# A two-layer transformer on one NeuronCore: two weight splits, the four-bit weight parts, the zeroing of the experts' rows and a count product in other places

## The reference

```python
def _L0_attn_ref(x, Wq, Wk, Wv, Wo):
    q = jnp.einsum('bsd,ed->bse', x, Wq)
    k = jnp.einsum('bsd,ed->bse', x, Wk)
    v = jnp.einsum('bsd,ed->bse', x, Wv)
    kvt = jnp.cumsum(k * v, axis=-2) * denom
    vhat = q * kvt
    return jnp.einsum('bse,fe->bsf', vhat, Wo)
...
# _L0_ffn_ref: a shared expert of 352 columns, and 8 experts of 176 columns of which each token takes 2
scores = jax.nn.sigmoid(xf @ gate_w.T)
topk_w, topk_idx = jax.lax.top_k(scores, TOP_K)
shared_out = jax.nn.silu(xf @ shared_wg.T) * (xf @ shared_wu.T) @ shared_wd.T
...
routed_out = (topk_w[..., None] * picked).sum(axis=1)
return (shared_out + routed_out).reshape(B, S, D)
...
# _L1_ffn_ref: weights stored in four bits, with a scale for each 32
vals = NVFP4_LUT[idx]
vals = vals.reshape(N, K // block, block) * scales[:, :, None]
...
x = L0_attn_x
xn = _layernorm(x, axis=-1)
x = x + _L0_attn_ref(xn, ...) + _L0_ffn_ref(xn, ...)
xn = _layernorm(x, axis=-1)
x = x + _L1_attn_ref(xn, ...) + _L1_ffn_ref(xn, ...)
```

## Time and profile before

| | us |
|---|---|
| median of 3 executions | 723.02 |
| lowest, highest | 722.76, 724.7 |
| the profiled execution | 726.48 |
| its span in the profile | 724.7 |
| PE busy | 666.8 |
| DVE busy | 503.4 |
| ACT busy | 391.8 |
| POOL busy | 364.0 |

### The profile page before, as it was taken

The page is one execution under the profiler, slowest core; times in us unless marked ns, Lnnn a source line. Parts: engine busy times, 40 slices in busy tenths (PEclk is TensorE's granted clock), DMA queues, the critical chain, the costliest instruction groups (busy, mean ns, idle before and its releaser), DMA issues.

```text
span 724.7 us, 12634 instructions
## 1 busy us (share of the span) xinstructions
PE 666.8 (92%) x4346; PEld 524.1 (72%) x4346; DVE 503.4 (69%) x964; ACT 391.8 (54%) x691; POOL 364.0 (50%) x299
## 2 busy tenths in 40 slices
PE   7999978899979799999899999999999989999996
PEld 4877756888878677776577767667777767776774
DVE  6888696558656858583966686495858487568755
ACT  4654323456544654753855492675465286449273
POOL 2333874857565734462646264364537163426453
PEclk9999998999999999999999999999999999999999
DMA  8527585698876567020024021003303000302100
GB/s 306 175 97 231 167 297 190 209 305 267 281 232 218 199 226 233 16 74 2 1 74 124 9 56 35 1 2 119 85 5 84 2 1 30 75 15 53 36 2 30
DMA packets 66802, 82.72 MB, mean 114 GB/s; under 512 B 7090, under 2 KB 50354, under 8 KB 66738
## 3 DMA queue, kind: packets, MB, share of 16 engines
q1 hardware_dynamic: 63156, 73.39, 32.0%
q0 software_dynamic: 3072, 8.39, 3.6%
q10 hardware_dynamic: 512, 0.13, 0.1%
HBM read 40.34 MB, written 28.84 MB: 95 GB/s over the span
## 4 chain that ended last, share of the span: by engine, by line
PE 54%; DVE 15%; issue 10%; ACT 10%; SPq 4%; POOL 2%; DMA 2%; another core or an unknown queue 1%; ACTq 1%; DVEq 0%; POOLq 0%
PE acc L660 4%; PE acc L662 4%; PE acc L661 4%; PE ring L660 3%; PE pm L662 2%; PE pm L661 2%; PE pm L660 2%; PE ring L661 2%; PE ring L1001 2%; PE ring L662 2%; PE ring L1007 2%; SPq L623 2%; PE pv L660 2%; PE pv L662 2%; PE pv L661 2%
## 5 line engine op out<-in xcount | busy, mean ns | idle before, releaser
L1606 POOL TENSOR_TENSOR hl<-hf,hh 128x512 fp32r<-128x512 f32 (+1 forms) x76 | 101.3, 1335 | 227.2 <-ACT hh L1286 226.8
L1286 ACT ACTIVATE hh<-hf 128x512 fp32r<-128x512 f32 (+1 forms) x76 | 47.6, 630 | 78.7 <-DVE hf L2160 60.8
L660 PE MATMUL acc<-hh,wh 128*128 128x512 f32 (+1 forms) x168 | 71.8, 427 | 2.9 <-POOL hl L1606 2.9
L2224 DVE TENSOR_REDUCE mx<-ring 128x2 f32<-128x512 f32 (+1 forms) x96 | 61.5, 682 | 8.4 <-PE ring L1007 8.4
L662 PE MATMUL acc<-hl,wh 128*128 128x512 f32 (+1 forms) x168 | 66.2, 394 | 0.0
L661 PE MATMUL acc<-hh,wl 128*128 128x512 f32 (+1 forms) x168 | 66.2, 394 | 0.0
L2160 DVE TENSOR_TENSOR hf<-hf,pv 128x512 f32<-128x512 f32 x64 | 43.6, 681 | 30.6 <-PE pv L662 26.1
L1751 POOL TENSOR_TENSOR pl<-act,ph 128x512 f16<-128x512 f32 x32 | 42.1, 1316 | 36.5 <-ACT ph L1501 29.7
L1478 ACT ACTIVATE hf<-pm 128x512 f32<-128x512 f32 x56 | 33.4, 596 | 43.2 <-PE pm L662 37.4
L660 PE MATMUL pv<-xh,wh 128*128 128x512 f32 x128 | 53.5, 418 | 0.0
L662 PE MATMUL pv<-xl,wh 128*128 128x512 f32 x128 | 50.6, 395 | 0.0
(11 more groups left out here) (294 smaller groups left out, 2047.1 us busy)
## 6 DMA issues: line engine op xcount, KB each, us to landing
w4s<-w4hl SPq DMA_DIRECT2D x16, 512.0 KB
ws<-qs SPq DMA_DIRECT2D x12, 512.0 KB, 5.4
qT<-qp SPq DMA_DIRECT2D x96, 64.0 KB
kT<-kp SPq DMA_DIRECT2D x96, 64.0 KB
xs<-yg SPq DMA_DIRECT2D x2, 2944.0 KB, 12.7
ys<-act SPq DMA_DIRECT2D x22, 256.0 KB
stage<-w SPq DMA_DIRECT2D x8, 608.0 KB, 4.9
xh<-xs SPq DMA_DIRECT2D x12, 256.0 KB
```

The costliest lines, as they stand in the source:

```text
L660: pe.matmul(o, w_hi, x_hi, start=first, stop=False, skip_group_check=True)
L1286: a.activation(h_parts(n)[0][0:rows, :], hf[0:rows, n % 2, :], ACT.Copy).then_inc(s_hh, 1)
L1606: return pool.tensor_tensor(dst, src, hi.bitcast(F32), ALU.subtract)
L2224: v.tensor_reduce(mx[:, i, h0:h0 + nh], ring[j % 2][:, :].rearrange("p (n k) -> p n k", n=nh), AX.X, ALU.max).then_inc(s_mx, 1)
```

## The change

Five things move. (1) The lo parts of pieces 11 and 12 are made by VectorE instead of GpSimd: 11 with piece 10 in group 1, 12 in group 2 behind `gated` of tile 1. (2) GpSimd's `w4_parts(0)` waits until the lo parts of the fourth group's vhat are there (`s_vhl`), and the parts 0 to 3 stand one place later each among the splits and scatters; `codes(0)` and the first two `scales_hi` come earlier, in group 2, tile 1, and `codes(4)` and `codes(5)` two steps of the loop later, `w4_out` of 1 to 5 likewise. (3) `clear(0)` is issued ahead of `piece(12)`. (4) GpSimd's first four tiles of rows go out together, then two, then two. (5) `counts(1)` stands ahead of `shared_down(3, 0)`, before it stood behind it.

```diff
-        lo_of = {0: [0, 2, 4, 6, 8, 10, 14], 1: [1, 3, 5, 7, 9, 11, 12, 13]}
+        lo_of = {0: [0, 2, 4, 6, 8, 10, 11, 12, 14], 1: [1, 3, 5, 7, 9, 13]}
...
             piece(11)
-            piece(12)
             sp.wait_ge(s_zero, 1)
             clear(0)
+            piece(12)
...
             w4_out(0)
-            w4_out(1)
...
-                    w4_out(2)
+                    w4_out(1)
                     rows_load(4)
...
-                if q in (4, 7, 10):
-                    w4_out(q // 3 + 2)
+                if q in (4, 5, 10, 11):
+                    w4_out(2 + q % 2 + q // 10 * 2)
...
+                if g == G - 1:
+                    counts(1)
                 shared_down(g, 0)
                 if g < G - 1:
                     qkv(g + 1, 0, 0)
-                if g % HG == 1:
-                    counts(g // HG)
+                if g == 1:
+                    counts(0)
...
+                    if g == 2 and t == 1:
+                        scales_hi(0)
+                        scales_hi(1)
...
-                if g == 2:
-                    scales_hi(0)
-                    scales_hi(1)
...
-                if q == 1:
+                if q == 3:
                     scales_hi(2)
...
-            rows_out_to(0, 0, 1)
-            weights(11)
-            rows_out_to(0, 2)
+            rows_out_to(0, 0, 1, 2, 3)
             split_h(6, ST_M[0])
-            rows_out_to(0, 3, 4)
+            rows_out_to(0, 4, 5)
             split_h(7, ST_M[1])
             split_h(8, ST_M[2])
-            weights(12)
-            rows_out_to(0, 5, 6, 7)
-            pool.wait_ge(s_wlo[1], lo_of[1].index(12) + 1)
+            rows_out_to(0, 6, 7)
+            pool.wait_ge(s_wlo[0], lo_of[0].index(12) + 1)
+            pool.wait_ge(s_wlo[1], lo_of[1].index(9) + 1)
+            pool.wait_ge(s_vhl, 2 * G)
             w4_parts(0)
+            split_h(9, ST_M[0])
             w4_parts(1)
-            split_h(9, ST_M[0])
-            w4_parts(2)
             split_h(10, ST_M[1])
             split_h(11, ST_M[2])
             rows_out_to(1, 0, 1)
+            w4_parts(2)
             w4_parts(3)
-            rows_out_to(1, 2, 3)
+            rows_out_to(1, 2, 3, 4, 5)
             w4_parts(4)
-            rows_out_to(1, 4, 5)
             w4_parts(5)
             rows_out_to(1, 6, 7)
...
-                        weights(10)
+                        weights(10, 11)
...
+                    if g == 2 and t == 1:
+                        weights(12)
+                        codes(0)
                     if g == 2 and t == 2:
-                        for k in range(4):
+                        for k in range(1, 4):
                             codes(k)
...
-                if q in (2, 3):
-                    codes(q + 2)
+                if q in (4, 5):
+                    codes(q)
```

## The result

| | before | after |
|---|---|---|
| median of 20 executions, us | 722.61 | 718.72 |
| lowest, highest | 719.33, 728.3 | 716.64, 721.87 |
| the profiled execution, its span | 726.48, 724.7 | 718.85, 717.0 |

The changed kernel takes 0.9949 of the time of the kernel before, with a 95% interval of 0.9931 to 0.9968: 3.9 us less by the medians. The forecast was 5.7 less, at 717.3, and its range of 714.3 to 720.2 holds 718.72. Single executions of either kernel spread over 5 to 9 us, so a difference of 1 or 2 us between two profiles says something only where the rows show its place.

The account below looks back on a forecast made before the run. TensorE (busy 92%) bounds the kernel, so time is won only where it waits or runs slowly; 4.2 + 2.5 + 0.8 - 0.6 - 0.3 - 0.9 = 5.7 us off 723.0 gives 717.3, range 714.3 to 720.2.

Parts of the forecast that it names:

- Bound and place: TensorE bounds; in group 3 near 104 to 114 us, a 4.2 us wait and 2.5 us of slow matmuls go.
- `weights(11)`, gain 0.8, loss 0.6: Split moved to VectorE: the `hf` wait goes, gain 0.8 us; slots and `residual(1)` come later, loss 0.6 to 1.0.
- `split_h(7)`, loss 0.3 within 0 to 1.0: Near 89 us: TensorE's 0.4 us wait stays; the split may meet VectorE's `codes(1)` to `codes(3)`, loss taken 0.3 us.
- `counts(1)`, 0: Count product 1.4 us sooner before the experts: worth 0, since the scan L1893 waits for GpSimd's run to end.
- The loop, loss 0.9 within 0 to 2.5: Expert loop: stores ahead of `codes_in(4)` bring the fifth scale block 1.7 us later; loss taken 0.9 us.
- The counts pay after all: Rival, before the experts: L1893 slips into GpSimd's 0.1 us gap, scan over 1.3 us sooner; 716.4 us, chance 0.12.
- `shares(1)`: Rival, near 107 us: L1881 waits for GpSimd's `split_h(9)` and `w4_parts(1)`, last splits 1.4 us later; 718.7 us, chance 0.14.
- The change doesn't do what it says: Rival: VectorE, with 2.8 us more work in groups 1 and 2, stays behind, vhat at 108; 723 us, chance 0.04.
- Slower: Rival, expert loop: ScalarE waits for the fifth scale block and stops the experts; 726 us, chance 0.04.
- The sum: All terms together: 5.7 us less than 723.0, so 717.3 us; 716.1 with losses at best, 720.0 at worst.
- The zeroing: `clear(0)` moves from 57.51 to about 44.6 us; slots near 68.4, not its DMA, then set GpSimd's scatter start.
- The signs it named: Group 3: no scan above 1 us, clock near 1.0; L1893 still stretched. Wrong: ScalarE waiting above 3 us in the loop.

Follow-up runs that it names:

- parts_alone: Kernel before with only the four-bit parts moved behind the fourth group's sums, with their stores and codes; both weight splits stay on GpSimd: 720.47 us, ratio 0.9960.
- before_again: The kernel before, unchanged, run again for a second profile: 723.74 us.
- w11_late: Changed kernel with VectorE's weights(11) behind residual(1) instead of in front of offsets(0): 725.62 us on chip B, ratio to before 0.9978.
- rows_late: Changed kernel with the first half's scatters of tiles 4 and 5 behind GpSimd's splits 7 and 8: 716.88 us, ratio to before 0.9902.
- counts_back: Changed kernel with counts(1) back behind shared_down(3, 0): 721.60 us, ratio to before 0.9972.
- lock: Changed kernel with a measurement in front: VectorE instructions released during GpSimd's run of four multiplications; VectorE's small products took 1248 ns in the median.
- ws_again: Changed kernel with the fourth and fifth block of codes issued ahead of the stores of parts: 728.47 us on chip C, ratio to before 0.9978.

## Why the prediction held, and where it was off

- **Bound and place.** Right. The 4.2 us of wait measured 4.36, the slow matmuls behind it 2.53 against 2.5, the wait for `hf` is gone. The `s_vhl` wait takes the four-bit parts out of VectorE's way: parts_alone gets the 4.2 and the 2.5 with that part of the change only. before_again shows that the slow clock was no accident of one profile.
- **`weights(11)`, gain 0.8, loss 0.6.** The gain measured 1.03, and parts_alone, which leaves this split on GpSimd, keeps the 0.8 us wait for `hf`. The loss measured 0.84 at 64.8, 0.96 with what follows to 66; inside its own bounds of 0.6 to 1.0. w11_late gets 0.86 of it back.
- **`split_h(7)`, loss 0.3 within 0 to 1.0.** Measured 1.28, and by another cause. The prediction said that TensorE's 0.4 us wait "stays" since two tiles of scatters lie ahead of the split as before. GpSimd began that split at 88.00 before and at 88.53 now, though it began the one ahead of it 0.7 us sooner: two of the four issues between them, beside VectorE's work, took 1.99 and 1.22 us instead of about 0.97. And TensorE arrives 0.9 us sooner. The split was set by GpSimd's row of issues, not by the hi copy, and so what TensorE had won at 80 us it waited for at 89. rows_late shows it.
- **`counts(1)`, 0.** The step that failed: it was put at nothing, and it is 1.9 us at the first expert tile, and 0.9 by the clock against the first profile. The prediction saw that the scan would stand ready at a gap of 0.1 us and gave that 0.12, because it took the path to be given back only at a run's end. counts_back and lock show the opposite. The rule rested on fewer cases than it says ("three of three cases", "up to three"): the run at 76.16 was one instruction, the scan at 120.08 met only the last one of its run, and both fit a hold of one instruction. Only L1947, through four, and L2019, through three, speak for the whole run. The place was right, the rule wrong.
- **The loop, loss 0.9 within 0 to 2.5.** 2.4 us against the second profile of before, 0.6 against the first: the size is not settled better than that. The prediction named one load, the fifth block, for which ScalarE waits 4.0 us, more than the 3 us that it named as a sign of being wrong. But the second profile of before has 3.15 us of this wait, against the 1.10 that the prediction started from, and ws_again takes the wait away and wins nothing. So the mechanism of this term, the block's place in the queue, is not confirmed. What takes the time instead stays open: the transfers as a whole in full DMA engines, or the two stores a step apart.
- **Rivals.** *The counts pay after all*, with a chance of 0.12, is what came. `shares(1)` was not lost: L1880 took 0.17 us, at 108.21, 0.46 us ahead of GpSimd's split. *The change doesn't do what it says* fell. *Slower* did not come; a loop that stretches is part of what took the gain down, but not by the load that the rival named.
- **The sum.** Two errors met. At the front the changed kernel is 8.0 us ahead of the second profile, 7.3 without the start's clock, where the prediction had 6.6 (4.2 + 2.5 + 0.8 - 0.6 - 0.3). Against the first profile it is 7.6 without the start's clock: 1.9 us won at the experts where the prediction had none, 0.4 more at the two waits it had, and 1.3 more lost than it had at the two splits. Then the loop takes 2.4, not 0.9, and 0.7 go near 205 us and behind it. That leaves 4.9 with the start's clock and 4.2 without, and the medians differ by 3.9; the second profile lies 1.1 above the median of before. The range held partly by luck, because these errors have opposite signs: without `counts(1)` counts_back measured 721.60, above the range.
- **The zeroing.** As predicted, GpSimd's first scatter (67.77 instead of 71.09) now waits for the slots and no longer for the DMA. No run has this part or the grouping of the scatters alone.
- **The signs it named.** No long scan, no wait above 1 us between 90 and 112, a clock of 1.00: all seen. The wait of 1.77 us stands at 88.1 to 89.85, just outside the stretch it named. The first expert matmul "at 118 to 120" came at 117.36; "L1893 still stretched" was wrong; the loop stretched by 2.4 against the one profile, just short of the 2.5 at which the forecast was to fail.

## What to carry to other kernels

A microsecond won on the critical path ends at the next engine that was just in time: list for each wait the one that stood behind it by less than the gain, here GpSimd's split at 88.0. Before a long wait for one load is taken as the loss, look whether the unchanged kernel has it in a second profile, and whether the time falls when it is taken away: here the unchanged kernel had 3.15 us of it, and the time did not fall. Where VectorE and GpSimd share a path, the turn between two instructions is mostly enough for the other one, so when an instruction becomes ready is worth more than how long it is. A run of GpSimd's right behind one of its DMA issues is the place to look first when VectorE is held longer.

## What the runs showed of the chip that I had not expected

- VectorE's and GpSimd's instructions on SBUF alternate one by one when both have some queued (1.7 us each for 0.68 and 1.26 alone), also when both begin with the same event. Nineteen instructions don't follow this, among them 5.4 and 5.9 us in the kernel before and 3.29 in the changed one, and in all of them GpSimd's run stood within 0.03 us behind an indirect DMA issue.
- The kernel before takes 722.6 to 723.4 us in two comparisons, 727.8 on chip B and 729.6 on chip C, and the change gains 0.9949 (0.9931 to 0.9968) in the first and 0.9980 (0.9954 to 1.0006) on C. On C ScalarE could go on only 10 us after a store of 256 KB was issued with four transfers of 512 KB behind it, and TensorE, which had idled, then ran at half clock.
- The first 26 us have a mean clock of 0.93 in some profiles and 1.00 in others; it moves all that follows by 0.7 to 0.9 us.
